# First pass of a graph kernel: counts per bin summed on TensorE from one-hot tiles, ranks made three blocks ahead in six parts

## The reference

```python
x = inputs["x"]                                   # 6250 x 64
ea = edge_attr_16 @ emb_ea                        # 206250 x 64
msg = relu(x[src] + ea)
s = segment_sum(msg, dst, num_segments=6250)
cnt = segment_sum(ones, dst, num_segments=6250)
x1 = relu(s / maximum(cnt, 1)[:, None] @ Wl0 + bl0 + x @ Wr0)
...
aggr = segment_sum(x[dst] * edge_attr_64, dst)    # third network, its sum of edge_attr_64 is taken in the first pass too
```

## Time and profile before

| | |
|---|---|
| median of 3 runs | 11810.08 us (11804.13 to 11818.93) |
| span of the profiled execution, first to last instruction | 11780.1 us |
| PE busy | 8643.6 us (73%) |
| DVE busy | 8144.6 us (69%) |
| POOL busy | 7991.9 us (68%) |
| ACT busy | 4536.2 us (39%) |
| mean granted TensorE clock | 0.674 |

### The profile page before, as it was taken

One profiled execution on the slowest core, in us unless ns is written; L12 is line 12 of the kernel. 1 busy time (PEld: TensorE's weight loads), 2 busy tenths in 40 slices (PEclk: granted clock), 3 DMA queues, 4 the chain that ended last, 5 costly groups with the idle time before them and its releaser, 6 DMA issues. The chain is left out here.

```text
span 11780.1 us, 261186 instructions
## 1 busy us (share of the span) xinstructions
PE 8643.6 (73%) x87631; PEld 7424.1 (63%) x87632; DVE 8144.6 (69%) x23580; ACT 4536.2 (39%) x10976; POOL 7991.9 (68%) x8039
## 2 busy tenths in 40 slices
PE   4778777779989799976666666666666666666665
PEld 3677766757878687855555556455555545555554
DVE  6777777779989754566666666666666666666667
ACT  2333333334444355533333333333333333333332
POOL 6666666637757475727777776577777747777773
PEclk9887888889999898965555555555555555555555
DMA  4555555538989686823333333233333323333332
GB/s 135 176 176 172 170 174 178 174 106 243 255 222 259 188 267 207 268 82 94 95 96 95 96 95 81 77 96 95 96 96 96 96 61 96 95 96 95 96 95 52
DMA packets 1292517, 1602.61 MB, mean 136 GB/s; under 512 B 245241, under 2 KB 1050836, under 8 KB 1290939
## 3 DMA queue, kind: packets, MB, share of 16 engines
q1 hardware_dynamic: 729130, 945.56, 25.7%
q0 software_dynamic: 254464, 283.59, 12.7%
q10 hardware_dynamic: 307600, 356.66, 10.4%
HBM read 1300.07 MB, written 284.81 MB: 135 GB/s over the span
## 5 line engine op out<-in xcount | busy, mean ns | idle before, releaser
L2230 POOL DMA_INDIRECT rows<-gat_table,wgt x2457 | 2338.9, 952 | 962.1 <-issue 747.8
L2230 POOL DMA_INDIRECT Y<-gat_table,wgt x2394 | 2279.5, 952 | 729.6 <-issue 729.6
L961 POOL DMA_INDIRECT bins<-scratch,slots x1288 | 1321.9, 1026 | 714.6 <-issue 551.1
L2243 PE MATMUL scores<-ident,rep 128*128 128x128 f32 x2436 | 610.9, 429 | 1080.0 <-ACT rep L2326 1080.0
L2243 PE MATMUL scores<-ident,scratch 128*128 128x128 f32 x2415 | 605.5, 428 | 1041.2 <-ACT scratch L2326 1041.2
L1309 ACT ACTIVATE xT<-xT 112x256 f32<-112x256 f32 x1716 | 711.5, 415 | 1658.6 <-DVE xT L1146 1391.9
L2284 PE MATMUL bank<-sel,msg 128*72 128x32 f32 x9702 | 1308.6, 309 | 0.0
L2284 PEld LDWEIGHTS bank<-sel,msg 128*72 128x72 f32 x9702 | 1215.6, 237 | 44.5
L1029 PE MATMUL bank<-xT 112*64 112x120 f32 (+1 forms) x13728 | 1173.5, 281 | 28.1 <-ACT xT L1309 27.8
L2243 PEld LDWEIGHTS scores<-ident,rep 128*128 128x128 f32 x2436 | 471.8, 223 | 1136.3 <-ACT rep L2326 1136.3
L1141 DVE TENSOR_TENSOR xT<-counts,xT 112x480 f32<-112x480 f32 x1716 | 1115.0, 650 | 84.8 <-issue 55.4
(11 more groups left out here) (280 smaller groups left out, 19069.5 us busy)
## 6 DMA issues: line engine op xcount, KB each, us to landing
work<-in_dst_rows SPq DMA_DIRECT2D x693, 448.0 KB
xT<-bins ACTq DMA_DIRECT2D x1716, 119.0 KB
work<-adj SPq DMA_DIRECT2D x184, 780.0 KB
work<-near_table SPq DMA_DIRECT2D x1118, 128.0 KB
near_table<-work SPq DMA_DIRECT2D x598, 128.0 KB
xT<-near_table SPq DMA_DIRECT2D x598, 128.0 KB
adj<-work ACTq DMA_DIRECT2D x299, 240.0 KB
bins<-zeros ACTq DMA_DIRECT2D x46, 1547.0 KB, 8.6
```

Of the source, the lines that this page charges most:

```text
L961: nc.gpsimd.indirect_dma_start(bins, bass.IndirectOffsetOnAxis(slots[u % 2][:, r * G + j:r * G + j + 1], 0), binf[r][:, j, :], None).then_ ...
L2230: nc.gpsimd.indirect_dma_start(rows[s][:, j, :], None, gat_table, bass.IndirectOffsetOnAxis(edge_sources[:, g * G + j:g * G + j + 1], 0)). ...
L2243: last = nc.tensor.transpose(score_banks[s % 2][:, j * P:(j + 1) * P], reps[s % 2][:, j, :], ident[:])
```

## The change

In the first pass, for each block:

- `totals`, `in_bins` and the semaphore `bins_counted` go, with the reduction L1205 and the copy L1206. PE sums the counts itself: 28 matmuls of `earlier16` with the 28 column tiles of `hot`, accumulated in one place of PSUM (`rank_event`, in step 3). `rank_sum` moves from bank 0 to bank 6, beside the sum of the plain groups, and `plain_sums` now also waits for the slot list.
- The ranks are made `RANK_LEAD` = 3 blocks ahead and not 2. Packing and scattering stay 2 ahead. There are three slot lists.
- `split` and `place` are cut into six parts, each at the end of a DVE step: `divide` (step 0), `describe` (1), `same_bins` (2), `sooner_in_bins` (4), `earlier_in_bins` (6) and `place` (7). Several waits of the chain inside them go (`link.mark` in place of `link`).
- Source numbers are loaded three blocks ahead; before the first body three blocks are ranked and not two.

```diff
-            rank_sum = bank[0][:, G * D:G * D + TS]
+            rank_sum = bank[6][:, D:D + TS]
...
+            def ranked_ahead(b):
+                return first_pass and b + RANK_LEAD < B
...
                         wait(pe, (q["msg_ready"], n + 1), (q["sel_ready"], n + 1),
-                             *([(q["accumulated"], before["group", n - 1] + 1)] if n else []))
+                             *([(q["accumulated"], before["group", n - 1] + 1)] if n else []),
+                             *([(q["slot_ready"], min(n + RANK_LEAD + 1, B))] if first_pass else []))
...
+                    def rank_event(b):
+                        n = b - RANK_LEAD
+                        wait(pe, (q["bins_hot"], b + 1), (q["slot_ready"], b),
+                             *([(q["accumulated"], before["group", n - 1] + 1)] if n > 0 else []))
+                        for j in range(GT):
+                            last = nc.tensor.matmul(rank_sum, earlier16[:], hot[:, j, :], start=j == 0, stop=j == GT - 1)
+                        last.then_inc(q["ranked"].handle, 1)
+
                     def bin_event(b, u, r):
                         m = GB * b + r
-                        if r == 0:
-                            wait(pe, (q["pay_ready"], m), (q["bins_counted"], b + 1))
-                            nc.tensor.matmul(rank_sum, earlier16[:], in_bins[:], start=True, stop=True).then_inc(q["ranked"].handle, 1)
                         wait(pe, (s_attr_bin[r], 16 * (b + 1)), (q["pay_ready"], m),
-                             *([(q["slot_ready"], b + 1)] if r == 1 else []), *([(q["rows_free"], b - LEAD + 1)] if r == 2 else []))
+                             *([(q["rows_free"], b - LEAD + 1)] if r == 2 else []))
...
-                        link(nc.vector.tensor_reduce(totals[:], hot[:].rearrange("p j t -> p t j"), AX, ALU.add))
-                        nc.vector.tensor_copy(in_bins[:], totals[:]).then_inc(q["bins_counted"].handle, 1)
...
+                    def rank_part(b, i):
+                        if i == 0:
+                            divide(b)
+                        elif i == 1:
+                            describe(b)
+                        elif i == 2:
+                            same_bins(b)
+                        elif i == 4:
+                            sooner_in_bins(b)
+                        elif i == 6:
+                            earlier_in_bins(b)
+                        elif i == 7:
+                            place(b)
...
-                            if first_pass and binned_ahead(b):
-                                if i == 0:
-                                    split(*ahead[:2])
-                                if i == at_bin[0] + 1:
-                                    place(*ahead[:2])
...
+                            if ranked_ahead(b):
+                                rank_part(b + RANK_LEAD, i)
```

More of the change, by code:

```diff
@@ L1184, in plain_event, with divide @@
                             plain_accumulate(n - 1)
[L1186 to L1188 removed]
+                    LINKS = 6 + 2 + 3
+                    def divide(b):
                         link.offset = LINKS * b
[L1190 to L1191 removed]
+                        wait(ve, (s_ids[b % 2], 16 * (b // 2 + 1)), (q["ranked"], b))
+                        link(nc.vector.tensor_scalar(quot[:], ids[b % 2][:], 2521, None, ALU.mult))
@@ L1207, in split @@
[L1207 to L1213 removed]
+                        link.mark(nc.vector.tensor_scalar(remb[:, :], rem[:, :], blockbase[:, ds(b, 1)], None, ALU.add))
@@ L1214, in place, with earlier_in_bins @@
+                    def earlier_in_bins(b):
+                        wait(ve, (q["ranked"], b + 1))
+                        link.mark(nc.vector.tensor_tensor(both[:, :, 0:TS], bc(rank_sum, [P, GT, TS], 1), hot[:], ALU.mult))
+                    def place(b):
+                        link.join()
+                        wait(ve, *[(s_binned[r], 16 * G * (b - RANK_LEAD + 1)) for r in range(GB)])
                         link(nc.vector.tensor_reduce(ranks[:, :], both, AX, ALU.add))
-                        nc.vector.scalar_tensor_tensor(slots[u % 2][:], ranks[:, :], float(TS), remb[:, :], ALU.mult, ALU.add
+                        nc.vector.scalar_tensor_tensor(slots[b % RANK_LEAD][:], ranks[:, :], float(TS), remb[:, :], ALU.mult, ALU.add
```

68 lines of the change are left out of this document (34 added, 34 removed).

## The result

| | before | changed |
|---|---|---|
| median | 11807.1 us (4 runs, 11799.76 to 11818.93) | 11622.4 us (4 runs, 11613.72 to 11639.01) |
| span of the profiled execution | 11780.1 us | 11624.9 us |
| end of the first pass in it | 2567.4 us | 2409.0 us |
| pace, mean of the last 39 block intervals | 53.2 us | 49.35 us |

The ratio is **0.9847, 95% interval 0.9833 to 0.9861**: 185 us faster by the medians, where 218 were forecast. Between the two profiled executions it is 155 us, and the first pass alone gives 158 of it; the rest of the program did not move. In the first pass 3.3 us come from its beginning (the first scatter starts at 81.82 and not at 85.12) and the rest, 155 us over 43 blocks, from their pace. So the question of the study is the pace: it was to fall by 5.0 us per block and fell by 3.9.

The account below looks back on a forecast made before the run. The prediction took PE and DVE waiting for one another as the bound, at 53.1 us per block. 43 blocks x 5.0 us plus 3 at the start gave 218 us, hence 11592 us; range 11515 to 11710.

Parts of the forecast that it names:

- What bounded the kernel before: Whole loop: no engine full; DVE's bursts `split` and `place` starve PE, PE's flushes idle DVE; 53.1 us per block.
- The `join` of step 0: DVE, step 0: `join` can follow `fetch` at once, 6.1 us earlier in the even block, 4.9 in the odd.
- Steps 0 to 3: Stretch between `join` of steps 0 and 4: gain 0.0 to 4.9 us even, 1.5 to 6.4 odd, by parts hidden.
- The second gain: PE's flush of step 3: evenly fed, it runs at the higher clock, 2.65 us instead of 5.04.
- Steps 4, 6 and 7: DVE's late parts cost 0 to 2.6 us; `place` and the wait of `plain_sums` cost nothing behind PE's flush.
- No idle DVE above 2 us ahead of the `join` of step 8: Sign of being right in the profile after: DVE idles at most 2 us before that `join`.
- The granted clock: Sign of being right: granted clock in the first pass near 0.95, from 0.87 in the window before.
- The sum: Per block: even gains 3.5 to 11.0 us, odd 3.8 to 11.3; POOL's limit 46.4; 5.0 taken as mean.
- POOL becomes the bound: Rival, POOL's indirect DMAs: they slow to 49.0 us per block, gain 4.1 us, 11631 us; chance 0.18.
- The attribute loads: Rival, PE's waits for attribute loads: doubling from 118 us, they cut the gain to 2.4 us, 11704 us; chance 0.12.
- Weights: Rival, step 3: each of the 28 matmuls pays its weight load, 2.8 us; gain 3.0 us, 11678 us; chance 0.03.
- step 8: Rival: PE stands in step 8 waiting for late DVE parts, up to 9.4 us per block, 11996 us; chance 0.03.

Follow-up runs that it names:

- b_rows_by_sync: Kernel before, with the 7 gathers per block taken off POOL and fixed rows loaded by SP instead: ratio 1.0005, pace 53.0 us.
- b_loads_early: Kernel before, with the attribute loads issued a turn earlier in SP's queue: ratio 0.9918, pace 52.1 us.
- b_counts_pe: Kernel before, with only the counts per bin moved to PE as 28 matmuls, `split` and `place` left whole, two blocks ahead: ratio 0.9890, pace 50.4 us.
- a_loads_early: Changed kernel, with each attribute load issued one place earlier in SP's queue: ratio 0.9811, pace 48.15 us.
- a_rows_by_sync: Changed kernel, with the 7 gathers per block taken off POOL and fixed rows loaded by SP instead: ratio 0.9820, pace 48.3 us.
- a_twice_28: Changed kernel, with the 28 matmuls of the counts run twice, 56 per block: ratio 0.9858, pace 49.2 us.
- a_double_store: Changed kernel, with every near tile stored a second time, to a second table, on SP's queue: ratio 0.9963, pace 51.9 us.

## Why the prediction was right, and where its sizes were off

The forecast of 11592 us came out at 11622, inside the range, and the direction and its mechanism hold. That it came so close is in part luck: between the profiled executions the gain is 155 us and not 218, and the mean of even and odd blocks hides that the odd ones fell out of their forecast. By its own steps:

- **What bounded the kernel before.** Right in that bursts of DVE starved PE: PE's waits for DVE's `join` fell by 158 us, and `b_rows_by_sync` shows POOL had no part in it. Incomplete in that the attribute loads were taken to be covered by `split`: they cost the old kernel 1.2 us per block (`b_loads_early`).
- **The reduction.** 2.9 us, and 2.9 us per block were gained by taking it away alone (`b_counts_pe`).
- **The `join` of step 0.** Right; it stands close behind its `fetch`, with 3.1 to 3.9 us of idle DVE ahead of it, so PE is what limits it there.
- **Steps 0 to 3.** The gain was counted as between 0.0 and 4.9 us even, 1.5 and 6.4 odd. On average it was 0.7 us even and a loss of 2.2 odd: the parts are exposed there. The `join` of step 1, behind `divide`, came 3.4 us (even) and 1.9 us (odd) after its `fetch`, where it had been 1.0 and 0.6. And the odd block, whose stretch before took 14.1 us on average and not the 15.8 of the one that was read, had less to gain. The second gain, the clock of the flush of step 3, is there in part: its 24 matmuls took 4.00 us on average over the pass before and 2.97 us after, 1.0 us less. The 28 matmuls mostly took 1.40 us and not 0.8: 32 of the 43 groups of the loop took that whole time and 38 at least 1.17, so they ran wholly or mostly at the lower clock, at which the prediction had put them at 1.6, and it took the value at the higher one (0.89 in `b_counts_pe`).
- **Steps 4, 6 and 7.** From step 4 to step 8 the even block lost 1.0 us and the odd one 1.8, within the 0 to 2.6 allowed. `place` is nearly hidden: the `join` behind it comes 0.4 us after its `fetch` in the even block and 0.2 in the odd one, on average. The wait of `plain_sums` for the slots is 1.0 us in the whole pass:

```profile
L1054 PE MATMUL bank<-sel,msg 128*65 128x32 f32 x658 | 47.4, 225 | 1.0 <-DVE slots L1237 1.0
```

- **No idle DVE above 2 us ahead of the `join` of step 8.** Right in the even blocks, wrong in about half of the odd ones. There it is not ranking that is late but PE, by a load and the flush at the lower clock behind it.
- **The start.** 3 us forecast, 3.3 measured at the first scatter.
- **The granted clock.** 0.90 in the window of 200 us where 0.95 was expected (over 200 to 2000 us it rose from 0.85 to 0.89); the flush of step 7 even got slower, 3.75 us on average before and 4.15 after, because the longer waits for loads stand ahead of it.
- **The sum, which is the step that was off.** The term was 5.0 us per block, with POOL's limit at 46.4 from a mean of 1.026 us for every one of its DMAs. By kinds, 3.5 to 11.0 us were forecast for an even block and 3.8 to 11.3 for an odd one; 5.6 and 1.8 came, so the odd block missed its range. With the early loads its gain is 5.8 us (41.3 us per odd block in `a_loads_early`), so most of what it missed are those waits; the even block, in which DVE then waits for gathered rows, gives 1.9 us of that back. The loop by itself gained 4.7 to 4.9 (`a_rows_by_sync`). But POOL's term was mis-sized: 28 scatters of 1.079, 7 gathers of 1.172 and the gaps are 49.0 us, 2.6 more than 46.4, and 1.05 us of the 4.9 were lost to it. The gathers' own row was in the trace of before with 1.048, so a small part, 0.2 us per block, could have been read; the rise of the means between the two kernels could not.
- **From the pace to the median.** The sum was made against the profiled span and carried over to the median with the 30 us between them. In the changed kernel the profiled execution's time, 11626.7 us, lies within 5 us of its median. That offset was scatter of one execution, and it is why the medians show 185 us and the profiles 155.

Of the rivals, **POOL becomes the bound** (49.0 us per block, 11631 us) is what came: its 49.0 us of POOL's work per block are what is measured, and its time is met within 9 us, by a mean of the 35 DMAs that is 0.07 above the scatters' before. Its second reason, that DVE's instructions and POOL's lock each other out, is isolated by no run; the traces hold the association told above, which fits it. Its first, denser traffic, is not borne out as the main cause. **The attribute loads** happened too: their waits did nearly double, 113.9 to 215.1 us. They did not add 2.6 us on top: removed alone they gave 1.2 us, and with POOL out of the way 0.9. The sign of being wrong that the prediction had set on them, waits well above 118 us, was there. **Weights** did not happen (`a_twice_28`), nor did **step 8**. With 0.60 on the plain forecast and 0.18 on POOL I had the likelier two the wrong way round: a limit at 46.4 that stands 1.7 us under the forecast pace of 48.1 asks for its durations to be read in both groups and with some growth.

By the Trainium skill (TensorE: Matmul & The Clock Gate, Part 1) an idle PE falls back to 1.2 GHz and regains 2.4 by staying busy. The trace agrees: the flush of step 7 ran at a mean granted clock of 0.59 and took 5.73 us behind a wait of 2.92, and it took 3.44 to 3.54 us in every block once the waits ahead of it were gone. The flush of step 12 ran slower instead, with PE's waits for DVE longer.

## What to carry to other kernels

Where two in-order engines hand work to one another step by step, a long burst on one ahead of what the other waits for leaves the other idle, and cutting it up and moving it behind that point gains even at equal work: this alone gave 2.6 us per block. Before putting a price on such a gain, add up each other engine's work per turn with its gaps, in separate groups, and expect the one that waits least to be next; here POOL stood at 49.0 us per block, the loop with its late loads at 48.3 and without them at 47.4, all close behind the bound that was removed. And look at what stands ahead of a load in its queue: a load whose buffer is free is still late when it is issued behind a store that waits for a late producer; one place earlier gave 1.2 us per block in either kernel.

## What was not expected of the hardware

POOL's shortest indirect DMAs of 128 rows took 0.94 us (gather) and 0.95 us (scatter) with 0.30 us between two, and the mean rose from 1.03 to 1.08 us (scatter) and from 1.05 to 1.17 (gather) between the two kernels, as POOL's own waits vanished. Single ones take up to 2.46 us, as in the timeline above, there the first gather behind the scatters. In `a_double_store`, with 12% more bytes per second than the changed kernel, neither mean was higher.

A small cost turned up on DVE. In the changed kernel `add_block` (the addition to `accT`) comes behind the small operations of `describe`, and its idle time grew from 0.9 to 33.0 us, 0.7 us in each block, ended by nothing that the profile shows:

```profile
L1176 DVE TENSOR_TENSOR accT<-accT,bank 65x120 f32 x46 | 12.7, 275 | 33.0 <-issue 33.0
```

What the engine's sequencer does in that time was not tried.
